# Layer norm on VectorE and turned x in the scan's own banks; adding transfers that wait two tiles back, at an expert's first tile one tile back

## What is computed

```python
xn = (x - mean(x)) / sqrt(var(x) + 1e-5)
zxbcdt = xn @ in_proj_w.T                      # z (1024), x/B/C (1280), dt (16)
xBC = silu(conv_b + sum(conv_w[:, k] * shifted(xBC, k) for k in range(4)))
dA_cs = cumsum(dt * A)                         # within a chunk
y = (C B^T * exp(seg(dA_cs))) @ (x * dt) + exp(dA_cs) * (C @ state) + x * D
state = state * exp(dA_cs[last]) + B^T @ (x * dt * decay)
y = y * silu(z);  y = y * rsqrt(mean(y * y) + eps) * norm_w
out = x + y @ out_proj_w.T
scores = xn @ w_gate_router.T; two best experts per token, softmax over the two
out += sum over the two of weight * (silu(xn @ gate.T) * (xn @ up.T)) @ down.T
```

## Time and profile before

| | us |
|---|---|
| median of 3 runs (847.73 to 849.02) | 848.38 |
| the profiled execution | 848.12 |
| its span, from the first to the last instruction | 846.3 |

### The profile page before, as it was taken

One profiled execution on the slowest core, in us unless ns is written; L12 is line 12 of the kernel. 1 busy time (PEld: TensorE's weight loads), 2 busy tenths in 40 slices (PEclk: granted clock), 3 DMA queues, 4 the chain that ended last, 5 costly groups with the idle time before them and its releaser, 6 DMA issues.

```text
span 846.3 us, 12470 instructions
## 1 busy us (share of the span) xinstructions
PE 670.4 (79%) x4157; PEld 544.9 (64%) x4158; DVE 516.8 (61%) x1047; ACT 372.7 (44%) x786; POOL 394.0 (47%) x326
## 2 busy tenths in 40 slices
PE   5684899799799699799799878448588887778780
PEld 5584777677677577587588667135376776666660
DVE  4973889569689689669668884356563333333320
ACT  3528565364464464464554552424163333333330
POOL 3411634634633643633644247874554444444431
PEclk9986999899999999999999989868889999999995
DMA  8423203303212212313213122913445554555542
GB/s 263 174 75 115 100 26 101 125 26 100 101 51 100 99 53 100 101 51 100 89 38 100 36 66 91 290 28 115 164 75 91 97 94 86 94 99 95 87 69 35
DMA packets 32833, 80.37 MB, mean 95 GB/s; under 512 B 5808, under 2 KB 10928, under 8 KB 30608
## 3 DMA queue, kind: packets, MB, share of 16 engines
q1 hardware_dynamic: 21520, 52.75, 18.7%
q0 software_dynamic: 9984, 21.09, 14.1%
q10 hardware_dynamic: 1280, 5.90, 2.3%
HBM read 60.42 MB, written 19.34 MB: 94 GB/s over the span
## 4 chain that ended last, share of the span: by engine, by line
PE 30%; DMA 28%; POOL 12%; DVE 12%; issue 11%; ACT 4%; SPq 1%; POOLq 0%; DVEq 0%; ACTq 0%
DMA out<-yo,tab 18%; PE pi L1340 14%; PE po L1365 5%; DMA e<-cs_d 5%; POOL tab_d L485 3%; DVE xs L896 3%; PE py L1412 2%; PE py L1405 2%; DMA xn_d<-xin 2%; DMA xg<-xn_d,tab 2%; PE pxb L1461 1%; POOL xin L451 1%; ACT m L651 1%; POOL ysq L469 1%; DVE ew L570 1%
## 5 line engine op out<-in xcount | busy, mean ns | idle before, releaser
L1340 PE MATMUL pi<-xh,whl 128*128 128x256 f32 x1152 | 177.2, 299 | 24.4 <-DVE xl L833 15.7
L1340 PEld LDWEIGHTS pi<-xh,whl 128*128 128x128 f32 x1152 | 157.7, 203 | 29.2 <-DVE xl L833 15.6
L896 DVE SCALAR_TENSOR_TENSOR xs<-raw,conv_w,xs 128x256 f32<-128x256 f32 x240 | 114.4, 539 | 21.8 <-ACT xs L629 21.8
L1365 PE MATMUL po<-wo,y 128*128 128x512 f32 x256 | 116.9, 610 | 8.0 <-issue 8.0
L542 POOL DMA_INDIRECT out<-yo,tab x39 | 62.0, 1590 | 111.3 <-DMA out<-yo,tab 94.9
L1340 PE MATMUL pi<-xl,whl 128*128 128x256 f32 x576 | 96.3, 291 | 0.0
L1365 PEld LDWEIGHTS po<-wo,y 128*128 128x128 f32 x256 | 49.1, 197 | 64.1 <-issue 63.9
L1340 PEld LDWEIGHTS pi<-xl,whl 128*128 128x128 f32 x576 | 83.2, 199 | 0.0
L651 ACT ACTIVATE m<-m,cs_tok 128x128 f32<-128x128 f32 x256 | 79.5, 389 | 0.5
L1496 PE MATMUL pg<-ew,xgh 128*128 x312 | 66.8, 357 | 0.7 <-DVE xgl L1220 0.7
L632 ACT ACTIVATE zs<-pi 128x512 f32<-128x512 f32 x32 | 19.1, 598 | 102.2 <-PE pi L1340 102.2
(11 more groups left out here) (203 smaller groups left out, 1282.8 us busy)
## 6 DMA issues: line engine op xcount, KB each, us to landing
m<-cs_d SPq DMA_DIRECT2D x16, 1024.0 KB, 5.0
e<-cs_d SPq DMA_DIRECT2D x32, 256.0 KB, 4.4
w_as_read<-in_w_in SPq DMA_DIRECT2D x9, 512.0 KB, 8.6
res<-in_x SPq DMA_DIRECT2D x16, 256.0 KB, 2.9
out<-o SPq DMA_DIRECT2D x16, 256.0 KB, 2.0
ew<-in_w_gu ACTq DMA_DIRECT2D x5, 768.0 KB, 8.1
xin<-in_x SPq DMA_DIRECT2D x6, 512.0 KB, 4.0
xn_d<-xin SPq DMA_DIRECT2D x6, 512.0 KB, 3.9
```

What stands on the lines that cost most here:

```text
L896: dve.scalar_tensor_tensor(out=xs[par][:, b, :], in0=raw[:, b, k:k + GT], scalar=conv_w[:, b, k:k + 1], in1=xs[par][:, b, :], op0=ALU.mult ...
L1340: mm = pe.matmul(bank[:, hf, :], whl[:, n, lo, k, hf * P:(hf + 1) * P], xx[:, k, :], start=k3 == 0, stop=k3 == 11)
L1365: mm = pe.matmul(po[:, :], y[:, b, :], wo[:, b, :], start=b == 0, stop=b == XB - 1)
```

## The change

Part one, the scan. The layer norm's small steps (`spread`) and the two 128x512 passes (`normalise`) go to VectorE; only the power to -1/2 stays on GpSimd (`root`, one instruction, now ahead of `sums` and `factor`). `statistics` and `spread` move ahead of the multiplication of `m`, `normalise` behind it. The turned x of groups 2 to 7 goes to the banks `pxb` and not to `pi`, `turn_group` moves ahead of `off(0)`, and `group_low` ahead of `decayed(1)`. The `pi` banks now simply alternate; the state matmuls, which write `pxb`, wait for `xl_done` (even tiles) or `lg_done` (odd tiles, where the router's output is in `pxb` as well). `count_picks` moves from the end of tile 12 to tile 13, into `pxb[1]`. At the start, VectorE's `weight_low(0)` stands ahead of `normalise(0)`.

Part two, the experts. Two tiles of one expert share no token, so an adding transfer needs only wait for those of earlier experts that could still be under way. VectorE computes a row `landed` with, for each j, how many additions of the other parity must have landed: those up to j-3, and at an expert's first tile those up to j-1. SP waits for that count and raises `may_add`; GpSimd waits for `may_add` and for add j-2. The padding rows of a tile get two sets of 128 rows, used in turn.

```diff
 def bank_of(g, n):
-    if g == 0:
-        return n % 2
-    return ((1, 0, 1, 0, 1, 1, 0, 1, 0) if g < G - 1 else (1, 0, 1, 0, 0, 1, 0, 1, 0))[n]
+    return (g * NP + n) % 2
...
+            def may(j, par, r):
+                if static(j, 1, 2):
+                    sp.wait_ge(y_out[1 - par], 16)
+                else:
+                    sp.wait_ge(y_out[1 - par], sp.value_load(landed[0:1, bass.ds(j, 1)], min_val=16, max_val=8 * J + 16))
+                sp.sem_inc(may_add, 1)
+
+            sp.wait_ge(eidx_done, 3)
+            for j in range(1, J):
+                may(j, j % 2, j // 2)
...
-            def layer_norm(q):
...
+            def root(q):
+                pool.wait_ge(veps_done, q + 1)
+                pool.tensor_tensor(rstdx[:, :], veps[:, :], nhalf[:, :], ALU.pow).then_inc(rstdx_done, 1)
...
+                if c == 0 and g + 2 < G:
+                    root(g + 2)
                 if t:
                     sums(t - 1)
...
-                if c == 0 and g + 2 < G:
-                    layer_norm(g + 2)
                 if t:
                     factor(t - 1)
...
-                    pool.wait_ge(y_out[(j - 1) % 2], 16 * ((j - 1) // 2 + 1))
+                    pool.wait_ge(may_add, j)
+                if j >= 2:
+                    pool.wait_ge(y_out[j % 2], 16 * (j // 2))
...
         def turned_half(q, half):
-            if q < 2:
-                return (pxb, py)[q][half][:, :, :].rearrange("p (k a) l -> p k (a l)", k=2)
-            return pi[half][:, :, :]
+            return (py if q == 1 else pxb)[half][:, :, :].rearrange("p (k a) l -> p k (a l)", k=2)
...
+            def spread(q):
+                st_q = stats[q % 2]
+                dve.wait_ge(bn_done, 2 * q + 2)
+                need(dve, rstdx_done, q)
+                need(dve, xn_done, 2 * q)
+                norm.step(dve.tensor_tensor(dif[:, :], st_q[:, :, 1], st_q[:, :, 4], ALU.subtract))
...
+            def normalise(q):
+                dve.wait_ge(rstdx_done, q + 1)
+                norm.after()
                 for c in range(2):
...
+                if c == 0 and prepares:
+                    statistics(g + 2)
+                    spread(g + 2)
                 dve.wait_ge(me, t + 1)
...
                 if c == 0 and prepares:
-                    statistics(g + 2)
+                    normalise(g + 2)
...
                 pe.wait_ge(xdd_done, t + 1)
+                if prepares:
+                    if c == 0:
+                        pe.wait_ge(xl_done, 2 * (g + 2) + 2)
+                    else:
+                        pe.wait_ge(lg_done, g + 3)
+                elif t == T - 3:
+                    pe.wait_ge(pos_read, 1)
...
-                if t == T - 4:
-                    count_picks()
```

More of the change, by code:

```diff
@@ L131, in block @@
         dt_tok = sb("dt_tok", [P, RING, HEADS])
+        landed = Area(nc, sb.at, top)("landed", [1, J], I32)
         conv_w, conv_b = sb("conv_w", [P, CB, TAPS]), sb("conv_b", [P, CB])
@@ L287, in block @@
         h_hi, h_lo, down, y_done = sem("h_hi"), sem("h_lo"), sem("down"), sem("y_done")
-        y_out = [sem(f"y_out{i}") for i in range(2)]
+        y_out, may_add = [sem(f"y_out{i}") for i in range(2)], sem("may_add")
         x_g = x.rearrange("(q t p) d -> q p t d", p=P, t=2)
@@ L1060, in experts_of_tiles @@
                 dve.tensor_copy(packed[:, :], pf[:, :]).then_inc(eidx_done, 1)
+                route.step(dve.tensor_tensor(ecmp[:, 1:J, 0], ef[:, 1:J], ef[:, 0:J - 1], ALU.is_gt))
+                route.after()
+                dve.wait_ge(lag_in_s, 16)
+                dve.wait_ge(ctap, 3 * CB * G)
+                route.step(dve.scalar_tensor_tensor(out=ecmp[:, 1:J, 1], in0=ecmp[:, 1:J, 0], scalar=16.0,
+                                                    in1=lag[:, 1:J], op0=ALU.mult, op1=ALU.add))
+                route.after()
+                dve.tensor_copy(landed[:, 1:J], ecmp[:, 1:J, 1]).then_inc(eidx_done, 1)
             dve.memset(ones[:, :], 1.0).then_inc(prep, 1)
@@ L1065, in vector @@
             statistics(0)
-            first_norm()
+            spread(0)
             weight_low(0)
+            normalise(0)
             group_low(0)
@@ L1073, in vector @@
             statistics(1)
+            spread(1)
             dve.wait_ge(c_in, 64)
@@ L1077, in vector @@
             weight_low(2)
+            normalise(1)
             stage(0, 0)
@@ L1179, in vector @@
                     time_steps(g + 2, 0, 2)
+                if c == 0 and prepares:
+                    group_low(g + 2)
                 decayed(1)
@@ L1183, in vector @@
                     stage(g + 1, n)
-                if c == 0 and prepares:
-                    group_low(g + 2)
                 if c == 1 and prepares:
@@ L1429, in tensor @@
                 stages(0)
-                if c == 1 and prepares:
-                    router(g + 2)
                 pe.wait_ge(btok_done, t + 1)
@@ L1435, in tensor @@
                 pe.matmul(pk_cb, xs[par][:, XB, tok], xs[par][:, XB + 1, tok], start=True, stop=True).then_inc(cbt, 1)
+                if c == 1 and prepares:
+                    router(g + 2)
+                if t == T - 3:
+                    count_picks()
                 stages(1)
@@ L1447, in tensor @@
                     rows_of(g + 1)
+                if c == 0 and prepares:
+                    turn_group(g + 2)
                 if t < T - 1:
@@ L1453, in tensor @@
                 diag(0)
-                if c == 0 and prepares:
-                    turn_group(g + 2)
                 if t == T - 1:
```

124 lines of the change are left out of this document (41 added, 83 removed).

## The result

| | before | after |
|---|---|---|
| median of 4 runs each, same chip, us | 848.23 (847.73 to 849.02) | 820.57 (818.08 to 825.91) |
| profiled execution, its span | 848.12, 846.3 | 818.08, 816.3 |

The ratio is 0.9681, 95% interval 0.9632 to 0.9731: faster by 27.7 us. Predicted were 815 and 800 to 832.

What follows compares the result with a forecast made beforehand. TensorE was taken to bound the scan, and additions throttling gathers through GpSimd's order the experts. From 848.12, experts -28.8, even tiles -4.5, start +1.5 and tile 13 -1.5 sum to -33.3: 814.8, forecast 815, range 800 to 832.

Steps and rivals of the forecast that it cites:

- The experts: Expert stage: 30 tiles save 28.5 us, first tiles cost 7, the end gives 7.3; sum -28.8 us.
- the loop: Experts: turn, result, addition, gather, turn through two tiles takes 9.40 us, 4.70 each, above TensorE's 4.48.
- first tiles: At an expert's first tile the wait stays one back: 1.15 us each, 6 in the stretch, +7 us.
- The end: Experts' end: without queued additions the last starts one result and hand-over behind TensorE, 7.3 or 7.4 us earlier.
- first rival: Experts: TensorE is the bound and first tiles cost nothing; stage -42.4 us, total 801; chance 0.12.
- Rivals 2, 4 and 5: Experts: longer gather loop, 831 (chance 0.17); additions in flight slow each other, about 867 (0.03); SP's permission late, 844 (0.04).
- The even tile: Scan: `finish` and `xl` come earlier, but waits mostly move; each tile gains 0.75 us, six tiles -4.5.
- Rival 3: Even tiles lose: `m` stays at 3.86 or the store lands later; +1.3 us each, total 827; chance 0.14.
- `m` by the shared port: Even tile: `m`, started after GpSimd's `xdd`, takes 2.29 us instead of 3.86, -1.57 a tile.
- The odd tile: Scan: the router's new wait for `xdt` is covered by `stages(0)`, 2.8 us; no change.
- The start: `normalise(0)` behind `weight_low(0)` delays the first turning 2.1 us; group 1's norm takes some back: +1.5 (0 to 2.1).
- Tile 13: TensorE's 5.24 us wait for `place` goes, as `count_picks` has its own bank; counted -1.5 (0 to -5.2).

Runs made afterwards that it cites:

- e2_relay_all: The kernel with the scan's change, every addition waiting one tile back as before the change, but through SyncE: 852.25 us, ratio 1.0093 to the kernel before.
- e3_gather_first: The changed kernel with a tile's gather issued on GpSimd ahead of the addition it stood behind: 799.17 us, ratio 0.9465 to the kernel before.
- e4_store_early: The changed kernel with the store of normalised x ahead of the other store in SyncE's queue: 788.34 us, ratio 0.9323 to the kernel before.
- the ten profiles: Profiles of the change and its variants without the edit of e8_norm_first: tile 0 starts at 59.9 to 61.8.
- e12_experts_alone: The kernel before with only the change's second part (additions two back, SyncE's permissions), nothing of the scan's: 822.18 us, ratio 0.9631 to the kernel before.
- e8_norm_first: The changed kernel with `normalise(0)` ahead of `weight_low(0)` on VectorE, as in the kernel before: 830.47 us, ratio 0.9747 to the kernel before.
- e11_again: The changed kernel itself run once more, unaltered: 828.16 us, ratio 0.9697 to the kernel before.
- e6_low_back: The changed kernel with `xl`'s two subtractions put back behind `decayed(1)`, `own(0)` and a conv stage: 848.98 us, ratio 0.9956 to the kernel before.
- e10_squares_late: The changed kernel with TensorE's sum of squares moved behind `turn_group` and `off(0)` in the even tiles: 827.01 us, ratio 0.9682 to the kernel before.
- e7_warm: The changed kernel with 22 useless matmuls filling TensorE's stall for `xl` in the even tile: 823.08 us, ratio 0.9657 to the kernel before.

## Why the prediction was right, and where it was wrong

- **The experts, right.** Predicted 4.70 a tile in the loop and 7 us for six first tiles, 148 for the stretch; measured 146.33. By the loop's own 4.70 the first tiles cost 5.3, 0.9 each, not 1.15, which fits that SyncE's relay, which I took at 0.3, is free (e2_relay_all). Steps of 4.1 and 5.4 by turns sum to the 9.40 that was worked out. e3_gather_first removes the loop and shows that it was the bound: 4.18.
- **The end, right.** Turn 38 to the last addition takes 13.8 where the earlier trace rows has 21.1, 7.3 less, by the value predicted.
- **No first rival, and why.** TensorE's floor was put at 4.48 and is 4.18. It was not reached, so the forecast didn't suffer; but with a floor of 4.45 I put e3_gather_first at 13 us less for these 30 tiles, and it was 146.33 - 125.49 = 20.8.
- **Rivals 2, 4 and 5, wrong.** Landings stay at 4.8, with DMA busy 0.62 of the time, 0.69 in e3_gather_first; SyncE's permission is waited for 3 times in 39.
- **The even tile, wrong.** Forecast were 0.75 us less, measured is none: 34.9 before and after. The waits were there: `m` at 2.29, VectorE idle 5 us, TensorE 3 us. From the start of tile 6 `finish` came at 19.7 where I had 19.1, and `xl` at 25.6 where I had 25.0. The step that failed is "the tile gains 0.75": it took the work behind the stall at its durations of tile 6 before (1.88 for the state matmuls, 1.09 for `diag(1)`), which ran at full clock; at 1.2 GHz they took 3.75 and 1.98, 2.8 more. I had no term for the clock at all, and did not see that four of the five even tiles before already ran in part at the lower level. And I had none for the sum of squares: that wait went from 1.1 to 2.1. On the mean of five tiles TensorE is busy 29.3 us instead of 29.0 and idle 5.5 instead of 5.9, so nearly all of the waiting came back. Rival 3 had a loss there, for reasons that came only in part: `m` ran at 2.29, but `xl` was late, by 0.3 to 0.6 in t = 2, 4 and 6, by 3.0 and 1.8 in t = 8 and 10.
- **`m` by the shared port, right.** The rule of the Trainium skill's page "SBUF — State Buffer", section "Who interferes with whom", held for `m`: 2.29 once `xdd` is over, and 3.87 in the odd tile t = 7 of the same kernel, beside `xdd`. The trace shows its other side too: GpSimd's `root`, two columns wide, takes 2.70 beside `m` where it takes 0.73 alone at the start, and VectorE's `normalise` waited 0.51 for it, which the prediction doesn't have.
- **The odd tile, wrong.** "The router's new wait for `xdt` is covered": it isn't. In t = 5, 7 and 9 the router waits 0.8 to 0.9, in the other three the first turning waits 0.35 to 0.6 for `carry` (the prediction had 1 us of that wait, as part of the even tile). Six odd tiles are 4.5 us longer. I had measured the cover by TensorE's 2.8 us of stages and not by when VectorE gets to `xdt` behind a conv stage. In e4_store_early no odd tile waits for `xdt`, all six wait 0.35 for `carry`, and they are 2.5 us longer than before.
- **The start, wrong.** The first turning came 2.1 later, as predicted, but tile 0 began no later: 60.18, and 59.9 to 61.8 in the ten profiles, against 61.27 before and 60.74 in e12_experts_alone. Forecast were +1.5. The order costs about 2.5 (e8_norm_first), so the rest of the change takes back as much; I had counted that as "takes back some". That it is group 1's norm, which no longer waits for GpSimd, is argued and not shown.
- **Tile 13, right in place, open in size.** `count_picks` no longer waits. Tiles 13 and 14 together take 71.7 before and 71.8 after, but 73.3 in e12_experts_alone against 71.7 in e11_again, so 0 to 1.6; I said 1.5.
- **The number.** 815 was forecast and 820.6 came. The scan, the start included, is about 10 us off, and the experts, 2.7 better than I said, hide a part of it. The time lies in the range because the scan's terms are small beside the experts', not because they were right.

## What to carry to other kernels

A forecast for a stall is not done when its length is known: ask what the clock will be behind it, and price the work there at that clock. Read the clock of several periods before taking one as the model; here the one chosen was the only one at full clock. When two transfers stand in one queue, look when each one's data is ready; here a store stood 10 us behind its data, and moving one call past another was worth about as much as the whole change. And in a loop that runs through an engine's program order, take the instruction that waits longest for others and put it last.

## What the runs showed of the hardware

- Two adding transfers that overlap by up to 1.7 us land as fast as one: 4.8 us in the median, before (at most one in flight) and after, and in e3_gather_first with DMA busy 0.69.
- A relay over a third engine (load of a number, wait for that value, increment, wait) cost nothing measurable on a path of 38 periods of 5.68 us.
- Behind TensorE's stalls in the even tiles the granted clock fell to 0.50 (1.2 GHz): in e6_low_back, e10_squares_late and e11_again behind each stall of 3.6 to 5.5 us at the state matmuls (of the tiles t = 2 to 10), behind waits of 2.1 to 2.9 in some. The kernel before had it too: four of its five even tiles ran at 0.92 or 0.95 on the mean. The price, up to 2.7 us, was nearly that of the stall. Useless matmuls in the stall prevented it there (e7_warm).
- The time that TensorE counts as busy overstates its need when it is starved: 4.48, 4.31 and 4.18 us a tile for the same instructions, the less the less it waited. Of the first step, 0.17, about 0.11 is the clock, an estimate from its 0.98 over 5.65 us; the second step is at 1.00 in both.
